# Linear attention of a four-stage kernel: project the output behind the norms, turn and decay the keys first, and reorder the inverse's steps on three engines

## What is computed

```python
q, k, v = (short_conv(h @ W, conv_w) for each)   # 4 taps over tokens, then silu
beta = sigmoid(h @ Wb)
g = -exp(A_log) * softplus(h @ Wa + dt_bias)
q = l2norm(q) * 32 ** -0.5 ; k = l2norm(k)       # 6 heads, keys of 32, values of 64
for each token:                                  # state S of 32 x 64 per head
    S = S * exp(g)
    S = S + k (x) ((v - k S) * beta)
    o = q S
o = o * rsqrt(mean(o * o) + 1e-5) * norm_weight * silu(h @ Wg)
x = x + o @ Wo
```

## Time and profile before

| | us |
|---|---|
| median of 3 runs | 1455.77 |
| lowest and highest | 1455.18, 1458.71 |
| the profiled execution | 1460.38 |
| its span, first to last instruction | 1458.8 |
| busy in the span: PE, DVE, ACT, POOL | 1208.2, 884.2, 623.8, 77.5 |
| mean granted clock of PE, share of full | 0.882 |

### The profile page before, as it was taken

One profiled execution on the slowest core, in us unless ns is written; L12 is line 12 of the kernel. 1 busy time (PEld: TensorE's weight loads), 2 busy tenths in 40 slices (PEclk: granted clock), 3 DMA queues, 4 the chain that ended last, 5 costly groups with the idle time before them and its releaser, 6 DMA issues. The chain is left out here.

```text
span 1458.8 us, 26683 instructions
## 1 busy us (share of the span) xinstructions
PE 1208.2 (83%) x10170; PEld 1012.2 (69%) x10170; DVE 884.2 (61%) x2570; ACT 623.8 (43%) x1591; POOL 77.5 (5%) x90
## 2 busy tenths in 40 slices
PE   4999999999899849998999875777768787786378
PEld 3888888788788738887888763556546565565255
DVE  3766457376375576665666766786576756653533
ACT  3634535454353334242424324554554545353221
POOL 1000000000000010000000001010110101100100
PEclk9999999999999959999999966687887886776699
DMA  8010000000000010000000011000000000000123
GB/s 262 1 59 1 1 2 1 0 0 0 0 1 1 24 56 1 1 1 2 1 1 1 13 35 49 27 25 2 27 1 27 26 2 26 1 2 2 49 93 112
DMA packets 25731, 34.12 MB, mean 23 GB/s; under 512 B 4781, under 2 KB 21005, under 8 KB 25613
## 3 DMA queue, kind: packets, MB, share of 16 engines
q1 hardware_dynamic: 25612, 32.52, 6.9%
HBM read 30.34 MB, written 2.17 MB: 22 GB/s over the span
## 5 line engine op out<-in xcount | busy, mean ns | idle before, releaser
L986 PE MATMUL b_ps<-ln_high,b_high 128*128 128x512 f32 x256 | 102.2, 399 | 26.4 <-PEq L61 20.9
L333 DVE TENSOR_REDUCE a_negmax<-a_ps 128x1 f32<-128x128 f32 x128 | 37.3, 291 | 116.3 <-PE a_ps L514 107.7
L986 PE MATMUL b_ps<-ln_low,b_high 128*128 128x512 f32 x256 | 101.9, 398 | 0.0
L986 PE MATMUL b_ps<-ln_high,b_low 128*128 128x512 f32 x256 | 101.7, 397 | 0.0
L889 DVE TENSOR_TENSOR gate_up_raw<-gate_up_raw,b_ps 128x512 f32<-128x512 f32 x64 | 43.3, 686 | 92.1 <-PE b_ps L986 60.0
L1013 PE MATMUL b_ps<-b_wd_high,b_mid 128*128 128x256 f32 x512 | 96.4, 283 | 0.0
L553 PE MATMUL a_ps<-a_wo_high,a_oT 128*128 128x256 f32 x512 | 94.7, 283 | 2.0 <-DVE a_oT L359 2.0
L945 ACT ACTIVATE gate_up_raw<-b_ps 128x512 f32<-128x512 f32 x64 | 37.5, 599 | 121.3 <-PE b_ps L986 121.2
L477 PE MATMUL a_ps<-ln_high,a_w_high 128*128 128x512 f32 x160 | 69.2, 432 | 15.6 <-PEq L61 15.6
L553 PEld LDWEIGHTS a_ps<-a_wo_high,a_oT 128*128 128x128 f32 x512 | 79.6, 188 | 2.8 <-DVE a_oT L359 2.8
L1013 PEld LDWEIGHTS b_ps<-b_wd_high,b_mid 128*128 128x128 f32 x512 | 80.6, 188 | 0.6
(11 more groups left out here) (376 smaller groups left out, 3183.4 us busy)
## 6 DMA issues: line engine op xcount, KB each, us to landing
d_slots<-in_D_packed SPq DMA_DIRECT2D x16, 433.0 KB, 4.6
c_a_all<-a_scratch SPq DMA_DIRECT2D x8, 768.0 KB
x<-in_hidden SPq DMA_DIRECT2D x4, 512.0 KB, 11.2
a_raw<-in_A_q SPq DMA_DIRECT2D x4, 512.0 KB, 8.5
gate_up_raw<-in_A_o SPq DMA_DIRECT2D x1, 2048.0 KB, 13.8
gate_up_raw<-in_B_g SPq DMA_DIRECT2D x1, 2048.0 KB, 12.1
gate_up_raw<-in_B_u SPq DMA_DIRECT2D x1, 2048.0 KB, 8.2
b_wd<-in_B_d SPq DMA_DIRECT2D x1, 2048.0 KB, 9.9
```

The source lines that it names most:

```text
L986: mm = nc.tensor.matmul(ps[:, bank, :], wpart, xpart, start=(j == 0), stop=(j == len(passes) - 1))
```

## The change

- Banks: INV32 (3, 2) becomes (3, 4), PART32 4 becomes 3, INV64 3 becomes 4, PART64 (2, 4) becomes (3, 2), INV128 (3, 4) becomes (4, 3).
- POOL: `decayed_keys` before `gated_outputs`.
- DVE: `keys_by_token` before steps 3 to 5; scans 0 to 2 before `fold_odd`, scans 3 to 5 behind steps 6 to 8; steps 9 to 11 before `keep_state`; more of the columns behind it; `mean_square` of half 1 and all later convolution steps sooner.
- ACT: `second_keys` behind `copy_part16`; `place_first` before `copy_part32`; `fold_even` and `place_off` before the copies of the turned output.
- PE: `turn_keys` behind `pair_part`; `scores` 4 before `quarter_part`; jobs 2 and 3 before `half_part`; `turn_low` 0 and 1 before `corner` and 2 right behind it; `all_norms`, then `outputs` of half 1, then `project_out`. The waits follow the banks.

```diff
--- before.py
+++ after.py
@@ -1585,7 +1585,7 @@
         n.start = 0

         NORM_BANKS, SCORE_BANKS, K_BANK, V_BANKS = (0, 1), (0, 1), 2, (5, 6)
-        PART16_BANK, INV32_BANKS, PART32_BANK, INV64_BANK, PART64_BANKS, INV128_BANKS = 4, (3, 2), 4, 3, (2, 4), (3, 4)
+        PART16_BANK, INV32_BANKS, PART32_BANK, INV64_BANK, PART64_BANKS, INV128_BANKS = 4, (3, 4), 3, 4, (3, 2), (4, 3)
         L_BANKS, SET_BANKS, O_BANKS, JOB_BANKS, GATE_BANKS = (0, 1, 2), (5, 6), (3, 5), (7, 7, 4), (2, 6)
         PAIRS = DH // 2
         TURNED_BANKS, DONE_BANK = (5, 6), 7
@@ -1687,8 +1687,8 @@
                 nc.gpsimd.memset(first[:], 0.0).then_inc(S["cleared"], 1)
                 queries(0)
                 for t in range(BATCH + 2):
+                    run(t, decayed_keys)
                     run(t - 2, gated_outputs)
-                    run(t, decayed_keys)
                     run(t + 1, queries)
 
             @block.vector
@@ -1846,52 +1846,46 @@
                     run(m, products, 2)
                     run(m, products, 3)
                     run(s, join_pairs)
+                    run(m, keys_by_token)
                     run(c, convolve, 3, 6)
                     run(m, products, 4)
                     run(m, products, 5)
+                    for h in range(3):
+                        run(c, scan, h)
                     run(m, fold_odd)
                     run(m, shuffles)
-                    run(m, column_product, 1)
-                    run(m, keys_by_token)
-                    run(m, column_sum, 1)
-                    for h in range(DH):
+                    run(m, columns, 1, 2)
+                    run(c, convolve, 6, 9)
+                    for h in range(3, DH):
                         run(c, scan, h)
-                    run(c, convolve, 6, 9)
-                    run(m, columns, 2, 4)
+                    run(c, convolve, 9, 12)
                     run(s, keep_state)
                     run(m, off_diagonal, 0)
+                    run(m, columns, 2, 3)
+                    run(m, off_diagonal, 1)
+                    run(m, columns, 3, 4)
+                    run(m, off_diagonal, 2)
                     run(m, columns, 4, 5)
-                    run(m, off_diagonal, 1)
-                    run(m, columns, 5, 7)
-                    run(m, off_diagonal, 2)
-                    run(m, columns, 7, 8)
                     run(s, second_values)
-                    run(c, convolve, 9, 10)
-                    run(m, columns, 8, 9)
-                    run(c, convolve, 10, 11)
+                    run(m, columns, 5, 9)
+                    run(c, convolve, 12, 13)
                     run(m, columns, 9, 10)
-                    run(c, convolve, 11, 12)
+                    run(c, convolve, 13, 14)
                     run(s, mean_square, 0)
-                    run(m, column_product, 10)
-                    run(c, convolve, 12, 13)
-                    run(m, column_sum, 10)
-                    run(c, convolve, 13, 14)
+                    run(m, columns, 10, 11)
+                    run(c, convolve, 14, 15)
+                    run(s, mean_square, 1)
                     run(m, column_product, 11)
-                    run(c, convolve, 14, 15)
+                    run(c, convolve, 15, 16)
                     run(m, column_sum, 11)
-                    run(s, mean_square, 1)
+                    run(d, add_out)
                     run(m, column_product, 12)
-                    run(c, convolve, 15, 16)
+                    run(c, convolve, 16, 17)
                     run(m, column_sum, 12)
-                    run(d, add_out)
-                    run(m, column_product, 13)
-                    run(c, convolve, 16, 17)
-                    run(m, column_sum, 13)
+                    run(c, convolve, 17, 18)
+                    run(m, columns, 13, 14)
                     run(c, keys)
-                    run(m, column_product, 14)
-                    run(c, convolve, 17, 18)
-                    run(m, column_sum, 14)
-                    run(m, columns, 15, 16)
+                    run(m, columns, 14, 16)
                     run(m, seeds)
                     if d == LAST:
                         n.sum_batches(dve, 2)
@@ -2087,11 +2081,14 @@
                         if inside(c):
                             channels.tap(act, c, j)
                     run(s, copy_part16)
+                    run(m, second_keys)
                     run(m, values_by_token, 0)
                     run(m, values_by_token, 1)
                     run(s, place_second)
+                    run(s, place_first)
                     run(s, copy_part32)
-                    run(s, place_first)
+                    run(m, fold_even)
+                    run(s, place_off)
                     if d == LAST:
                         n.copy(act, ps, 0)
                     run(d, copy_oT, 0)
@@ -2099,8 +2096,6 @@
                     if d == LAST:
                         n.copy(act, ps, 1)
                         n.copy(act, ps, 2)
-                    run(s, place_off)
-                    run(m, fold_even)
                     if inside(c):
                         channels.silu(act, c, 0)
                         channels.silu(act, c, 1)
@@ -2108,7 +2103,6 @@
                         channels.tap(act, c, 3)
                     run(s, copy_part64)
                     run(s, place_corner)
-                    run(m, second_keys)
                     run(s, copy_y, 0)
                     run(s, copy_y, 1)
                     if inside(c):
@@ -2171,7 +2165,7 @@
 
                     pe.wait_ge(S["kqg_ready"], at("kqg_ready", m, 2))
                     if m >= 1:
-                        pe.wait_ge(S["pc_copied"], at("pc_copied", m - 1, 1))
+                        pe.wait_ge(S["gate_taken"], at("gate_taken", m - 1, 1))
                     rows = KEYS - P
                     nc.tensor.transpose(ps[:, K_BANK, 0:P], kq[:, 0, 0, 0:P], r.ident[:])
                     nc.tensor.transpose(ps[:, K_BANK, P:KEYS], kq[0:rows, 1, 0, 0:P], r.ident[0:rows, 0:rows])
@@ -2194,6 +2188,7 @@
 
                     pe.wait_ge(S["aq_ready"], at("aq_ready", m, (5, 6, 6)[p]))
                     if p == 2:
+                        pe.wait_ge(S["kg_ready"], at("kg_ready", m, 2))
                         pe.wait_ge(S["ktok_ready"], at("ktok_ready", m, 1))
                     for u in range(2 * HALVES):
                         mm = nc.tensor.transpose(ps[:, L_BANKS[p], u * P:(u + 1) * P],
@@ -2240,7 +2235,6 @@
                             mm = nc.tensor.matmul(ps[rows, INV32_BANKS[0], cols32(u)], inv16[rows, u, :],
                                                   part16[rows, u, :], start=True, stop=True)
                     mm.then_inc(S["a_done"], 1)
-                    pe.wait_ge(S["gate_taken"], at("gate_taken", b, 1))
                     for u in range(UNITS):
                         for rows in QUARTERS[0:3]:
                             mm = nc.tensor.matmul(ps[rows, INV32_BANKS[1], cols32(u)], part16[rows, u, :],
@@ -2275,6 +2269,11 @@
                     if b == 0:
                         pe.wait_ge(S["cleared"], at("cleared", 0, 1))
                     pe.wait_ge(S["half_copied"], at("half_copied", b, 1))
+                    if b + 1 < BATCH:
+                        pe.wait_ge(S["kg_ready"], at("kg_ready", b + 1, 2))
+                        pe.wait_ge(S["ktok_ready"], at("ktok_ready", b + 1, 1))
+                    else:
+                        pe.wait_ge(S["gate_taken"], at("gate_taken", b, 1))
                     for i, us in enumerate(UNIT_SETS):
                         for u in range(us.start, us.stop):
                             mm = nc.tensor.matmul(ps[upper, PART64_BANKS[i], cols64(u)], low[lower, b % 2, u, upper],
@@ -2374,6 +2373,7 @@
                     run(c, job, 0)
                     run(c, job, 1)
                     run(s, pair_part)
+                    run(m, turn_keys)
                     run(m, scores, 2)
                     run(m, turn_values, 0)
                     run(m, turn_values, 1)
@@ -2382,33 +2382,32 @@
                         pe.wait_ge(S["saved"], at("saved", LAST, 2))
                         n.turn(pe, ps, r.ident, 0)
                         n.turn(pe, ps, r.ident, 1)
+                    run(m, scores, 4)
                     run(s, quarter_part)
                     run(d, turn_out, 0)
                     run(d, turn_out, 1)
                     if d == LAST:
                         n.turn(pe, ps, r.ident, 2)
-                    run(m, scores, 4)
                     run(s, quarter_inverses)
-                    run(s, half_part)
                     run(c, job, 2)
                     run(c, job, 3)
+                    run(s, half_part)
+                    run(m, turn_low, 0)
+                    run(m, turn_low, 1)
                     run(s, corner)
-                    run(m, turn_keys)
+                    run(m, turn_low, 2)
```

(7 more changed lines are left out.)

## The result

The changed kernel took **1369.81 us** in the median of 4 runs (1365.69 to 1379.87), the kernel before 1455.47 (4 runs on the same chip, 1453.52 to 1458.71): a ratio of **0.942** with a 95% interval of 0.937 to 0.946. Run again later, beside the experiments, it took 1367.01 (6 runs), ratio 0.939 [0.936, 0.942]. The forecast was 1395 in a range of 1370 to 1424: the direction holds and so does the main step, but the gain is 86 us instead of 61.

A forecast was written before the change was run, and what follows sets the result against it. No engine is full; a chain of waits behind projection and outputs bounds each round. Rounds of 25.5 + 2.4 + 20.3 = 48.2 us save 52.7 in rounds 2 to 6, 61.1 in all: 1395 us, range 1370 to 1424.

The forecast's parts named there:

- The chain: Between known and the next scores, projection and outputs hold up norms, ACT and DVE; norms would start 8.9 us sooner.
- rival 2: PE stays at its upper clock: rounds of 44 us, gain 86 us, kernel 1370 us; chance 0.14.
- T0 to T0': From PE's start of head 0's scores to the same moment one round later; forecast 46 to 50 us.
- The tail: DVE from second_values to the keys, 12.5 us; with the stretch before it, 20.3 us from solve's copy to T0'.
- The solve's copy: ACT's copy_y at T0+25.5, plus 2.4 us: half of the 4.8 us excess of the mean round over t = 3.
- ACT's order: place_first and fold_even before the copies: quarter inverses and place_off later, 2.4 us of cost on the inverse's chain.
- POOL: gated_outputs moved after T0: 2.3 us leave DVE's tail, no cost after T0; a long column 15 or seeds instead.
- Round 1: The round with full inverse but no output projection, 49.6 us before; forecast 48.2, a gain of 1.4 us.
- Round 7: The round without norms: a gain of 3 us from the excess and the turned keys, bounds 0 and 6.
- rival 1: The inverse becomes the bound through ACT's order and half-rate PE: rounds of 53 us, kernel 1420 us; chance 0.20.
- rival 3: Gain given back: squares of half 1 still wait, DVE's later order eats the rest; 1455 us, chance 0.04.
- rival 4: Slower: a chain of keys across all engines early in a round delays it if decayed keys come late; chance 0.06.

The follow-up runs named there:

- the doubled gates: PE's gate matmuls of the second half computed twice with the same result, against the changed kernel: 1361.98 us, 0.935 of the kernel before.
- the third kernel: The kernel before with PE's norms first and POOL's swap together, nothing else of the change: 1400.29 us, 0.961 of the kernel before.

## Why the prediction was right, and where it was off

**The chain.** Right. With the norms behind `known` both the 8.4 us wait of ACT and the 8.0 of DVE are gone, and the edit by itself is worth 38 us. PE's gap of 2.57 us lies in the 2 to 6 that were named. That the projection's own wait goes "since step 12 now comes before `keep_state`" shows in the kernel with PE's order undone: it loses 17 us, not 38.

**The range.** The direction and the chain were foreseen; that 1370 is held by the range is in part luck. The forecast's own range, 1380 to 1412, misses it, and so do all the bounds that it names taken at once (1375 to 1417). The lower end of 1370 came from rival 2, which had 0.14. T0 to T0' was to be 46 to 50 us and was 42.1 to 46.6 in rounds 2 to 6.

**The tail.** The step that was mis-sized most. From the solve's copy to T0' the forecast took 20.3; rounds 2 to 6 show 17.4, 18.1, 18.2, 17.4 and 18.2, 17.9 in the mean (17.4 in the second profile). Of the 2.4, 1.8 lie in DVE's tail, 12.5 by the sum, 10.7 by the rows (1089.52 to 1100.26). Columns 5 to 7 were charged at the mean column, 0.52 + 0.26, but that mean held the locked products and the wide columns; they took 1.84 us together, not 2.3. The queries were charged 0.8 for holding a product and held none by more than 0.1. The last 0.5 is an idle 0.50 us at the mean square that stood in the tail of t = 1, from which the sum started, and is gone. The remaining 0.6 are in the stretch before `second_values`: 7.25 us in t = 4, where 7.8 was in the sum. 5 x 2.4 = 12 us.

**The solve's copy.** Forecast at T0+27.9 with half the excess; measured 27.7, 26.1, 26.2, 24.6 and 28.4, mean 26.6 (25.0 in the second profile). 5 x 1.3 = 6.5 us. With the tail that is 18.5 of the 18.6 by which rounds 2 to 6 beat the forecast. The copy comes sooner than in the mean of before, 29.1, but not sooner than in its best round: t = 3 had it at T0+24.3 with a granted clock of 0.87, where t = 3 and 4 of the changed kernel, at 0.88, have it at 26.1 and 26.2. Which move makes that difference is not shown.

**ACT's order.** The times were right (quarter inverses at T0+15.6, 15.4 forecast; `place_off` at 17.6, as forecast), but the text called them the cost of the change, 2.4 us on the chain of the inverse. That fell: undone, the kernel is 15 us slower. The sum followed `fold_even` only up to `place_off` and not to the copy behind it, where the same 1.84 us stand in the old order.

**The clock.** Rival 2 gave 1370 and 44 us a round with PE at its upper level, and got 0.14. (Its 45.2 us "by the terms above with no excess" should be 25.5 + 20.3 = 45.8.) The time and the length of a round are the rival's, but not its reason alone: in the profile PE starts most rounds with 1.9 to 2.08 us of scores and is granted 0.82 to 0.92 of full speed. The argument against it ("PE would wait longer for DVE's keys") does not hold: PE's gap is 2.57 us in the changed kernel behind rounds of 42.1 and of 46.6 us alike, and with the doubled gates, at a granted clock of 0.96 to 1.00, rounds of 40 us keep a gap of 1.3. The Trainium skill, "TensorE: Matmul & The Clock Gate", section "What's actually happening", has activity release the throttle. The traces agree in the main, but PE's last gap alone doesn't decide. Behind gaps of 0.85 to 1.6 us the scores took 1.13 us in every round of these runs. Behind 2.6 us they took anything from 1.13 (at 1142.48) to 2.08, and behind 3.4 us as well: 1.48 to 2.08 in most rounds, and 1.13 once in the kernel with POOL's swap alone.

**POOL.** Right that 2.3 us leave the tail (column 12 at 0.42, the tail 2.2 us shorter in the third kernel), right, as far as the runs can tell, that `gated_outputs` costs nothing after T0, and wrong in what would be seen: the profile after has no long column 15 and no long seeds. Column 15 had been long before the change, 0.95 us in each round, beside `decayed_keys`, and is short after it (0.54), now that it starts 0.25 us sooner after T0. The Trainium skill, "SBUF — State Buffer", section "SBUF: two separate sides", has a DVE instruction of two SBUF inputs and a GpSimd one that reads SBUF lock each other out, and whichever starts first keep the other waiting for its whole length. The traces agree: DVE's seeds took 0.58 us when they started 0.13 us before POOL, and 1.67 when POOL was first by 0.8.

**The small terms.** Round 1 was summed at a full round's 48.2 us, though it has no projection and no `add_out`: it took 41.9, a gain of 7.7 and not 1.4. Round 7 won 0, where 3 were taken and 0 was the bound. Round 0 gave 0.5 (1.5 forecast), the rounds behind 7 gave 2.3 (2.5). Together: 0.5 + 7.7 + 71.3 + 0 + 2.3 = 81.8, where 61.1 was forecast; the two profiled executions lie 80.5 apart, the medians 85.7.

**Rivals 1, 3 and 4.** DVE's wait at `keep_state` is 2.5 us in the mean, under the 5 that would have spoken for rival 1, though one was 7.5. The keys reach PE at T0+7 with no wait of note, so the chain of rival 4 never binds.

**What stays open.** Why some rounds lose the upper level in their middle: in t = 6 of the profile after the scores took 1.13 us, and yet the round took 46.6 us at 0.82. The two profiles of the same kernel, at a mean clock of 0.903 and 0.915, are 9 us apart. Open too is whether the late matrix turns cost anything. How the parts add up is only bounded: norms first 38 us, POOL's order 6 alone and 19 on top of it, and the other 28 to 33 are the banks and the orders of ACT, DVE and PE's turns, of which ACT's is 15 when undone alone (20 against the second measurement).

## What to carry to other kernels

When several engines stand in a row behind work that only one of them needs, move that work behind the value they wait for, and follow each moved instruction to the end of the chain, not to the first place where it is late. Edits that shorten the idle time of TensorE need not add up: two that were worth 38 and 6 us alone gave 56 together, with the granted clock up from 0.78 to 0.84, where each alone had left it at 0.80 and 0.77. A mean duration that holds a few disturbed instructions should not price the quiet ones.

## What was not expected of the hardware

Work added to TensorE did not make the kernel slower and probably made it a little faster: 1.3 us more of gate matmuls a round (0.935 against 0.942 and 0.939, with intervals that just overlap), with scores of 1.13 us in rounds 3 to 7, where the changed kernel had 1.13 to 2.08. The effect is not safe to build on: with more of the same in two rounds the median was no better. And a distance of 0.13 us in the rows was enough to settle which of DVE and POOL went first; the other then waited.
